# Slot finding moved ahead of the first expert of a routed network, two of four shared-expert groups moved behind the last, and GpSimd's indirect DMAs issued by TensorE's step count

## The chip, the core and the metric

One core of a Trainium2 chip runs the whole program. The metric is the device time of one execution in microseconds (us), the median of three runs. The engines are TensorE (PE in the rows, its weight loads PEld), VectorE (DVE), ScalarE (ACT), GpSimd (POOL) and SyncE (SP, which issues most DMAs); each runs its own instruction list, and they meet through semaphores.

## What is computed

2048 tokens (8 sequences of 256, width 128) go through four stages, each with a LayerNorm behind it. The change touches the second, a mixture of experts:

```python
shared_out = swiglu(x, shared_w1, shared_w2)             # every token
gates = softmax(x @ wg.T)                                # 64 experts
w_topk, idx_topk = top_k(gates, 8)                       # 8 experts of each token, weights normalised
rank = place of the token among those of its expert      # in token order; kept if rank < 160
out = einsum(x1 * silu(x2), expert_w2), x1, x2 = split(buf @ expert_w1)   # buf: 64 experts x 160 slots x 128
x = layernorm(x + shared_out + sum of the kept rows, each times its weight)
```

The first stage is linear attention with running sums, the third four encoder layers, the fourth a block applied to the 192 best-scored of each 256 tokens. Everything is float32, with float16 for the exact small integers of the routing.

## The kernel before

**Stage 1 with the routing in it.** The tokens are handled in 4 groups of 512 (`GROUPS`), 4 tiles of 128 each. While TensorE and VectorE do the attention of group g, the routing of groups g-1 and g-2 is put between: logits (`route_logits`), best eight (`best_of`), masks, ranks (`ranks`, `split_ranks`). The last group's routing comes behind the attention. In the same place the shared expert runs: `shared_hidden(g, f)` on TensorE (L647, L648: two 512-column products for one of 3 blocks of one of 4 groups), Silu and a copy on ScalarE (`shared_halves`, L1056, L1057), the product on GpSimd (`shared_products`, L1298), and `shared_rows(g)` (L659, 24 matmul records), kept by ScalarE (L1061). The first expert waits for all four groups of it (L782).

**Finding slots.** For each set of 4 experts (a "Q", 16 of them) VectorE makes one-hot tables: `low_table` (L1629, 2048 float16 a partition) and `high_table` (three operations of 320: L1635, L1637, L1639). TensorE multiplies them for two Qs at a time (`find_slots`, L721, 64 matmuls), and VectorE turns the result into row numbers (`indices`, L1645 to L1655), which GpSimd's DMAs use. Q 0 to 5 have their tables, and Q 0 to 3 their indices, ahead of the first expert; the rest is done in the experts' loop: a table behind each step's product, and `find_slots` and `indices` in steps 1, 5, 9, 13, 17 and 21.

**The loop of 64 experts** (L785 on TensorE, L1127 on ScalarE, L1700 on VectorE). Step n of TensorE: the result of expert n-2 (`expert_result`, L778, 3 matmuls), one transposition (inputs of the next Q, `turn_inputs`, L748, in the second and third step of a Q; results of an earlier one, `turn_results`, L762, in the others), then the hidden layer of expert n (`expert_hidden`, L768, 6 matmuls, 12 records), which raises the semaphore `expert_mm`. That semaphore releases ScalarE's Silu (L1119), VectorE's copies (L1669) and SP's load of a later expert's weights (L441, 576 KB, a ring of 8). VectorE multiplies (L1681), which releases TensorE's result of that expert two steps later.

GpSimd carries the rows by indirect DMA, 5 blocks of 128 rows for each Q: `gather_block` (L1311) brings tokens and gates from DRAM into one of 4 buffers, `scatter_block` (L1318) puts weighted results (`rows_back`, L1692) back into DRAM. Its list is fixed: gathers of Q 0 to 5 first (`AHEAD = 6`), then, for each Q, five scatters of Q and five gathers of Q+6, one behind the other:

```python
for Q in range(NEG):
    for b in range(RB):
        scatter_block(Q, b)         # waits for back_read at b = 0 and 3
    if Q + AHEAD < NEG:
        for b in range(RB):
            gather_block(Q + AHEAD, b)
```

For Q 10 to 15 no gather is left; four of them have an addition of shared rows and tokens instead (L1344). `rows_back(Q, 0)` waits until the scatters of Q-3 have landed.

**Behind the loop** SP waits for all scatters and loads the returned rows (L453), VectorE and GpSimd sum them (L1738, L1439), and stage 3 begins.

## Time and profile before

| | us |
|---|---|
| three runs | 756.96, 752.38, 752.27; median 752.38 |
| the profiled execution's own time | 748.92 |
| its span, first to last instruction | 747.1 |
| TensorE busy | 583.6 (78%), mean granted clock 0.895 |
| VectorE, GpSimd, ScalarE busy | 454.8, 359.2, 235.2 |
| the loop of experts | about 162.5 to 406.4 of the span |

The chain of work that ended last is 58% TensorE, 15% VectorE, 8% "issue" (waiting for nothing that the profile shows) and 7% "another core or an unknown queue"; the kernel has one core, so the last name means a wait that ended on something that the records don't name. A busy share is an average over stages with different limits: what the change is worth has to be read from the stretches that it touches. Ends of matmuls are modelled.

### The profile page before, as it was taken

Reading aid. Unit: us, or ns where it says so; the run is one execution under the profiler, and the core shown is the slowest. Engines: PE = TensorE matmul, PEld = TensorE weight load, DVE = VectorE, ACT = ScalarE, POOL = GpSimd, SP = SyncE. Lnnn points to the kernel's source line nnn. Section 1 sums busy time; section 2 is a strip of 40 time slices with the busy share of each in tenths; the row PEclk is TensorE's granted clock in tenths of the full one; section 3 lists DMA queues with packets and bytes.
Section 4 is the critical chain, followed back from the end, with each engine's and each line's share of the span. In section 5 each row is a group of like instructions: output and inputs, shape, how many; then the busy total and the mean of one; then the engine's idle time right before and its main releaser. Section 6 shows DMA issues by size and latency. Waiting matters only on the chain.

```text
span 747.1 us, 11154 instructions
## 1 busy us (share of the span) xinstructions
PE 583.6 (78%) x3747; PEld 485.0 (65%) x3747; DVE 454.8 (61%) x1401; ACT 235.2 (31%) x447; POOL 359.2 (48%) x357
## 2 busy tenths in 40 slices
PE   6998877967958697979797032579999999999861
PEld 5767644666958586878796022458777877877641
DVE  4677655616646333323343268887778778777995
ACT  3133245212212122212232010134344344443564
POOL 4655122775465555666456449742243233234342
PEclk9998998879989899889899555689999999999995
DMA  8950000125555566657573660000000000000001
GB/s 306 415 218 22 22 8 21 43 64 180 155 183 170 178 202 202 212 187 236 194 226 95 254 267 1 0 1 12 4 29 11 4 28 11 4 28 1 1 2 57
DMA packets 29565, 79.43 MB, mean 106 GB/s; under 512 B 7104, under 2 KB 12096, under 8 KB 29264
## 3 DMA queue, kind: packets, MB, share of 16 engines
q1 hardware_dynamic: 23088, 65.69, 25.6%
q0 software_dynamic: 6432, 13.16, 6.0%
q8 instruction: 25, 0.41, 0.2%
q14 instruction: 20, 0.16, 0.1%
HBM read 62.60 MB, written 16.25 MB: 106 GB/s over the span
## 4 chain that ended last, share of the span: by engine, by line
PE 58%; DVE 15%; issue 8%; another core or an unknown queue 7%; ACT 4%; POOL 4%; DMA 2%; SPq 0%; DVEq 0%; POOLq 0%; ACTq 0%
PE bank L768 12%; PE bank L904 6%; PE bank L892 6%; PE bank L778 5%; PE bank L525 4%; PE bank L834 3%; PE bank L852 2%; PE bank L815 2%; PE bank L829 2%; DVE stats L253 2%; PE bank L843 2%; PE bank L870 2%; POOL rstd L268 2%; PE bank L557 1%
## 5 line engine op out<-in xcount | busy, mean ns | idle before, releaser
L268 POOL TENSOR_TENSOR rstd<-veps,minus_half 128x4 f32<-128x4 f32 x52 | 53.9, 1037 | 208.0 <-DVE veps L261 205.7
L768 PE MATMUL bank<-hidden,ring 128*128 128x160 f32 x768 | 126.7, 316 | 3.7 <-issue 2.6
L1318 POOL DMA_INDIRECT returned_rows<-x1t,scatter_all x80 | 81.0, 1013 | 81.7 <-DVE x1t L1692 62.5
L768 PEld LDWEIGHTS bank<-hidden,ring 128*128 128x128 f32 x768 | 116.5, 205 | 5.2 <-issue 3.7
L1119 ACT ACTIVATE hidden<-bank 128x480 f32<-128x480 f32 x64 | 36.9, 576 | 185.7 <-PE bank L768 136.3
L778 PE MATMUL bank<-hidden,ring 128*128 128x160 f32 x384 | 68.4, 315 | 19.7 <-DVE hidden L1681 16.4
L778 PEld LDWEIGHTS bank<-hidden,ring 128*128 128x128 f32 x384 | 58.3, 199 | 24.0 <-DVE hidden L1681 19.1
L1669 DVE COPY hidden<-bank 128x384 f32<-128x384 f32 (+1 forms) x32 | 23.3, 732 | 78.1 <-PE bank L768 55.1
L1170 ACT ACTIVATE arena<-bank,layer_cols 128x512 f32<-128x512 f32 x64 | 44.0, 687 | 62.6 <-PE bank L892 62.6
L815 PE MATMUL bank<-consts,arena 128*128 128x128 f32 x192 | 28.4, 284 | 44.1 <-DVE arena L292 44.1
L904 PE MATMUL bank<-ring,arena 128*128 128x128 f32 x512 | 59.9, 275 | 1.4 <-issue 1.4
L904 PEld LDWEIGHTS bank<-ring,arena 128*128 128x128 f32 x512 | 58.4, 192 | 2.4 <-issue 2.4
L892 PE MATMUL bank<-arena,ring 128*128 128x512 f32 x128 | 57.6, 592 | 0.0
L815 PEld LDWEIGHTS bank<-consts,arena 128*128 128x128 f32 x192 | 23.0, 145 | 47.3 <-DVE arena L292 41.5
L1681 DVE TENSOR_TENSOR hidden<-bank,hidden 128x480 f32<-128x480 f32 x64 | 41.8, 654 | 11.0 <-ACT hidden L1119 6.0
L1692 DVE TENSOR_TENSOR x1t<-bank,slot_gate 128x384 f32<-128x384 f32 (+1 forms) x32 | 15.5, 488 | 44.9 <-remote 28.5
L292 DVE TENSOR_SCALAR arena<-shared,mv,rstd 128x128 f32<-128x128 f32 x128 | 38.0, 360 | 7.8 <-POOL rstd L268 7.8
L1266 POOL TENSOR_TENSOR arena<-arena 128x512 f32<-128x512 f32 x30 | 32.7, 1127 | 12.5 <-DVE arena L1474 12.5
L892 PEld LDWEIGHTS bank<-arena,ring 128*128 128x128 f32 x128 | 23.2, 190 | 23.4 <-issue 23.3
L525 PEld LDWEIGHTS bank<-consts,arena 128*128 128x128 f32 x256 | 31.9, 201 | 7.2 <-issue 3.8
L1483 DVE TENSOR_TENSOR arena<-bank,arena 128x512 f32<-128x512 f32 x36 | 24.3, 685 | 19.8 <-PE bank L525 13.8
L1138 ACT ACTIVATE arena<-bank,layer_cols 128x512 f32<-128x512 f32 x16 | 12.4, 777 | 74.4 <-PE bank L815 74.4
(210 smaller groups left out, 1195.0 us busy)
## 6 DMA issues: line engine op xcount, KB each, us to landing
ring<-in_ew SPq DMA_DIRECT2D x64, 576.0 KB
returned_rows<-zeros SPq DMA_DIRECT2D x16, 512.0 KB, 14.9
arena<-returned_rows SPq DMA_DIRECT2D x6, 512.0 KB, 11.8
hidden<-returned_rows SPq DMA_DIRECT2D x4, 512.0 KB, 5.0
ring<-returned_rows SPq DMA_DIRECT2D x4, 512.0 KB, 7.9
ring<-in_l1w SPq DMA_DIRECT2D x8, 256.0 KB, 2.7
returned_rows<-x1t,scatter_all POOLq DMA_INDIRECT x80
shared<-in_xr SPq DMA_DIRECT2D x1, 1024.0 KB, 7.9
```

What stands on the lines that cost most here:

```text
L268: pool.tensor_tensor(rstd[:, s, :], veps[:, s, :], minus_half[:], ALU.pow).then_inc(sem(f"rstd{which}_ready"), 1)
L292: ins = v.tensor_scalar(dst[:, i, :], src[:, i, :], mv[:, s, i, 0:1], rstd[:, s, i:i + 1], ALU.subtract, ALU.mult)
L525: mm = pe.matmul(bank[3 + c % 3][:, tile_of(t)], A["kvp"][:, g % 2, t, P * e:P * e + P], cum, start=True, stop=True)
L768: mm = pe.matmul(bank[2 * (n % 2) + part][:, CAP * f:CAP * f + CAP], ring[:, n % RING, P * (FB * part + f):P * (FB * part + f) + P], E["xt ...
L778: mm = pe.matmul(bank[4 + n % 2][:, 0:CAP], ring[:, n % RING, P * (2 * FB + f):P * (2 * FB + f) + P], E["prod"][:, n % 2, CAP * f:CAP * f ...
L815: mm = pe.transpose(bank[b][:, P * t:P * t + P], src[:, t, :], ident)
L892: pe.matmul(bank[(3, 4, 6, 7)[f]][:], w_up[:, P * f:P * f + P], B["ht"][:, g], start=True, stop=True).then_inc(sem("up_mm"), 1)
L904: mm = pe.matmul(bank[5][:, P * t:P * t + P], B["relu"][:, g % 2, f, P * t:P * t + P], w_down[:, P * f:P * f + P], start=(f == 0), stop=(f ...
L1119: act.activation(E["silu"][:, n % 2, :], bank[2 * (n % 2) + 1][:, 0:FB * CAP], ACT.Silu).then_inc(sem("silu_ready"), 1)
L1170: act.activation(B["relu"][:, g % 2, f], bank[(3, 4, 6, 7)[f]][:], ACT.Relu, bias=layer_col(l, 5 + f)).then_inc(sem("relu_ready"), 1)
L1318: pool.indirect_dma_start(returned_dram[:, :], bass.IndirectOffsetOnAxis(ap=scatter_all[:, Q, b:b + 1], axis=0), E["back"][:, Q % BACK, b, ...
L1681: v.tensor_tensor(E["prod"][:, n % 2, :], bank[2 * (n % 2)][:, 0:FB * CAP], E["silu"][:, n % 2, :], ALU.mult).then_inc(sem("prod_g_ready"), 1)
```

## The change

1. All slots are found ahead of the first expert, in 5 calls (`FOUND`: one pair of Qs, one pair, then two pairs three times). The high tables are made in two wide calls (Qs 0 and 1; Qs 2 to 15) from codes and token numbers that ScalarE spreads out beforehand, in place instead of by way of `here`. The low tables of Qs 0 to 3 are made for the first 12 of 16 tiles while the last group's logits are under way. The loop loses its tables, its `find_slots` and its `indices`.
2. The shared expert: groups 0 and 1 stay ahead of the loop (`SOON = 2`), with the product on VectorE straight from PSUM instead of copy and GpSimd; groups 2 and 3 come behind the loop, and their bases are added by VectorE instead of GpSimd. `shared_hidden(0, 0)` moves behind the last group's attention.
3. GpSimd's list waits for TensorE's steps.

```diff
-        here = sb("here", [2, RB, TILES, EG], F16)
-        a_code, b_code, token16 = sb("a_code", [RA * EG], F16), sb("b_code", [RB * EG], F16), sb("token16", [TILES], F16)
+        a_code, b_code = sb("a_code", [RA * EG], F16), sb("b_code", [RB * NE], F16)
+        token16 = hidden[:, 3 * FB - 1].bitcast(F16)
...
+        SOON = 2
+        late = [B["kp"][:, m] for m in range(GROUPS)] + [B["eq"][:, m] for m in range(2)]
...
+        FOUND = ((0,), (1,), (2, 3), (4, 5), (6, 7))
...
-                if g == GROUPS - 1:
-                    shared_hidden(0, 0)
...
             attention_out(GROUPS - 1, 1)
+            shared_hidden(0, 0)
             shared_hidden(0, 1)
+            turn_x1(GROUPS - 1)
+            route_logits(GROUPS - 1)
             shared_hidden(0, 2)
-            turn_x1(GROUPS - 1)
+            ranks(GROUPS - 1)
             shared_hidden(1, 0)
-            route_logits(GROUPS - 1)
             shared_hidden(1, 1)
-            ranks(GROUPS - 1)
...
+            find_slots(0)
             shared_rows(0)
             shared_hidden(1, 2)
...
+            find_slots(1)
             shared_rows(1)
+            for call in range(2, len(FOUND)):
+                find_slots(call)
...
-            pe.wait_ge(sem("shared_ready"), GROUPS)
+            pe.wait_ge(sem("shared_ready"), SOON)
...
                 expert_hidden(n).then_inc(sem("expert_mm"), 1)
-                if j == 1 and Q + 2 < NEG // 2:
...
-                    find_slots(Q + 2, bank[6])
...
+            for g in range(SOON, GROUPS):
+                turn_late(g)
+            for f in range(FB):
+                late_hidden(SOON, f)
+            late_hidden(SOON + 1, 0)
+            late_rows(SOON)
+            late_hidden(SOON + 1, 1)
+            late_hidden(SOON + 1, 2)
+            late_rows(SOON + 1)
...
-            for b in range(RB):
-                gather_block(0, b)
-            shared_products(2)
-            for b in range(RB):
-                gather_block(1, b)
-            shared_products(3)
-            for Q in range(2, AHEAD):
+            for Q in range(AHEAD):
                 for b in range(RB):
                     gather_block(Q, b)
             pool.wait_ge(sem("zeroed"), 16 * TOK * TOPK // (8 * P))
+            def step(n):
+                pool.wait_ge(sem("expert_mm"), min(n + 1, NE + LAG))
+
             for Q in range(NEG):
-                for b in range(RB):
+                n = EG * Q + 2 * EG
+                step(n)
+                for b in (0, 1):
+                    scatter_block(Q, b)
+                step(n + 1)
+                for b in (2, 3, 4):
                     scatter_block(Q, b)
                 if Q + AHEAD < NEG:
-                    for b in range(RB):
+                    step(n + 2)
+                    for b in (0, 1):
                         gather_block(Q + AHEAD, b)
-                elif Q + AHEAD < NEG + GROUPS:
...
+                    step(n + 3)
+                    for b in (2, 3, 4):
+                        gather_block(Q + AHEAD, b)
```

VectorE's list ahead of the loop becomes, from the last residual on:

```diff
+            shared_product(0)
+            shared_product(1)
+            v.wait_ge(sem("codes_ready"), 2)
+            v.wait_ge(sem("bi_ready"), GROUPS - 2)
+            for Q in range(4):
+                low_table(Q, 0, KNOWN)
             best_of(GROUPS - 1)
             masks_of(GROUPS - 1)
             places_of(GROUPS - 1)
             split_ranks(GROUPS - 1)
+            v.wait_ge(sem("b_index"), GROUPS)
+            v.tensor_copy(group_of(bi16, GROUPS - 1), group_of(logits_i, GROUPS - 1)).then_inc(sem("bi_ready"), 1)
             invert_sums(GROUPS - 1)
...
+            high_tables(0, 2)
+            for Q in (0, 1):
+                low_table(Q, KNOWN)
+            indices(0)
+            for m in (2, 3, 4):
+                shared_product(m)
+            high_tables(2, NEG)
+            for Q in (2, 3):
+                low_table(Q, KNOWN)
+            low_table(4)
+            indices(1)
+            shared_product(5)
+            for call in (2, 3, 4):
+                for Q in range(4 * call - 4, 4 * call):
+                    if Q > 4:
+                        low_table(Q)
+                if call > 2:
+                    indices(call - 1)
+            indices(4)
```

Behind its last `rows_back`, VectorE adds the bases of groups 0 and 1, makes the 6 products of the late groups (`late_product`) and adds their bases; ScalarE has 2 copies and 6 Silus there, where it had none.

## Rows read from the trace of the kernel before

**Rows 1.** Stretches between Silus of steps 0, 8, 50, then loop end, scatters landed, rows in.
```profile
core 0: us, PE busy (x) PEld busy (x) DVE busy (x) ACT busy (x) POOL busy (x), PEclk, DMA share, GB/s
165.49:196.36 30.87, 25.25 (x219) 24.31 (x219) 19.12 (x45) 6.71 (x14) 12.34 (x13) 0.93 0.48 150
196.36:367.82 171.46, 135.70 (x991) 129.55 (x991) 69.16 (x152) 37.70 (x84) 104.80 (x105) 0.90 0.62 194
367.82:406.40 38.58, 37.72 (x281) 37.02 (x280) 17.15 (x34) 13.88 (x30) 20.64 (x20) 1.00 0.50 158
406.40:417.90 11.50, 0.02 (x1) 0.00 (x0) 0.73 (x2) 0.00 (x0) 7.86 (x8) 0.61 0.51 164
417.90:425.50 7.60, 0.00 (x0) 0.00 (x0) 0.65 (x6) 0.00 (x0) 0.00 (x0) 0.50 0.88 326
```

**Rows 2.** Stretch view of four steps, 368.79 to 379.67, with five scatters in them.
```profile
368.79:379.67 10.88, 10.88 (x84) 10.88 (x83) 4.77 (x10) 3.33 (x8) 6.22 (x6) 1.00 0.76 249
```

**Rows 3.** Waits of 196.36 to 367.82: engine line waited for, us, times, longest.
```profile
ACT hidden L1119 <- PE bank L768: 85.9, 25, 11.7
ACT hidden L1119 <- remote: 47.9, 10, 7.6
```

**Rows 4.** Timeline of all engines, 284 to 304 (start us, us, engine, line, operation).
```profile
288.28 1.80 PE L768 MATMUL bank<-hidden,ring 128*128 128x160 f32 x12
290.95 1.80 PE L768 MATMUL bank<-hidden,ring 128*128 128x160 f32 x12
293.22 0.95 POOL L1311 DMA_INDIRECT small<-dispatch_rows,gather_all  x1 [0.30 <-issue]
295.91 0.57 ACT L1119 ACTIVATE hidden<-bank 128x480 f32<-128x480 f32 x1 [7.63 <-remote]
297.23 1.97 PE L778 MATMUL bank<-hidden,ring 128*128 128x160 f32 x6 [4.48 <-DVE hidden L1681]
297.28 1.02 POOL L1318 DMA_INDIRECT returned_rows<-x1t,scatter_all  x1 [3.11 <-DVE x1t L1692]
299.63 3.41 PE L768 MATMUL bank<-hidden,ring 128*128 128x160 f32 x12
301.19 0.98 POOL L1318 DMA_INDIRECT returned_rows<-x1t,scatter_all  x1 [0.30 <-issue]
302.48 0.98 POOL L1318 DMA_INDIRECT returned_rows<-x1t,scatter_all  x1 [0.30 <-issue]
```

**Rows 5.** Timeline of GpSimd, the first scatter of the runs before and after.
```profile
281.65 1.02 POOL L1318 DMA_INDIRECT returned_rows<-x1t,scatter_all  x1 [3.25 <-DVE x1t L1692]
312.97 1.02 POOL L1318 DMA_INDIRECT returned_rows<-x1t,scatter_all  x1 [3.18 <-DVE x1t L1692]
```

**Rows 6.** Timeline, 97 to 162: what stands ahead of the loop.
```profile
99.15 1.05 PE L525 MATMUL bank<-consts,arena 128*128 128x128 f32 x8
100.24 0.69 DVE L1483 TENSOR_TENSOR arena<-bank,arena 128x512 f32<-128x512 f32 x1 [1.99 <-PE bank L525]
116.09 0.60 DVE L1519 MAX8 best<-logits 128x8 f32<-128x64 f32 x4 [7.87 <-ACT logits L1029]
123.44 2.09 DVE L1629 TENSOR_TENSOR arena<-zeros,a_code 128x2048 f16<-128x2048 f16 x1 [2.74 <-ACT zeros L1048]
154.51 5.40 PE L659 MATMUL bank<-sw,hidden 128*128 128x128 f32 x24 [4.35 <-POOL hidden L1298]
161.19 1.24 DVE L1669 COPY hidden<-bank 128x384 f32<-128x384 f32 x2 [12.76 <-issue]
```

**Rows 7.** The lines of the tables and of the shared hidden layer: ns min/median/max.
```profile
L1629 DVE TENSOR_TENSOR arena<-zeros,a_code x16: 1214/1216/2092, 123.4 to 242.3; 128x2048 f16<-128x2048 f16 x16
L1635 DVE TENSOR_TENSOR here<-zeros,b_code x16: 301/315/1380, 125.5 to 245.3; 128x320 f16<-128x320 f16 x16
L1637 DVE TENSOR_TENSOR arena<-here,token x16: 491/492/503, 126.9 to 245.7; 128x320 f16<-128x320 f16 x16
```

**Rows 8.** Timeline, 402 to 426: the end of the loop and what follows.
```profile
402.72 0.57 ACT L1119 ACTIVATE hidden<-bank 128x480 f32<-128x480 f32 x1 [0.92 <-PE bank L768]
415.64 0.98 POOL L1318 DMA_INDIRECT returned_rows<-x1t,scatter_all  x1 [0.30 <-issue]
425.53 3.69 DVE L1738 TENSOR_TENSOR hidden<-hidden 128x1536 f32<-128x1536 f32 x2 [6.86 <-DMA hidden<-returned_rows]
```

**Rows 9.** Timeline: a shared hidden product and the rows of a group, full clock.
```profile
136.83 1.02 PE L648 MATMUL bank<-x1t,sw 128*128 128x512 f32 x2
137.69 1.02 PE L647 MATMUL bank<-x1t,sw 128*128 128x512 f32 x2
143.78 2.94 PE L659 MATMUL bank<-sw,hidden 128*128 128x128 f32 x24 [1.70 <-POOL hidden L1298]
```

More of the change, by code:

```diff
@@ new lines, in find_slots @@
+            def find_slots(call):
+                if call >= 2:
+                    pe.wait_ge(sem("slots_read"), call - 1)
+                if call == 1:
+                    pe.wait_ge(sem("hidden_ready"), 4)
+                for k, q in enumerate(FOUND[call]):
+                    pe.wait_ge(sem("one_hots_ready"), 2 * q + 2)
+                    for u in range(2):
+                        at = 2 * RB * EG * (2 * k + u)
+                        lo = EG * (2 * q + u)
+                        for i in range(TILES):
+                            mm = pe.matmul(slot_bank(call)[:, at:at + 2 * RB * EG], a16[:, i, 2 * q + u, :],
+                                           b16[:, :, i, lo:lo + EG], start=(i == 0), stop=(i == TILES - 1))
+                mm.then_inc(sem("slots_mm"), 1)
@@ L1132, in _ @@
                     keep_result(n - LAG)
+            for g in range(SOON, GROUPS):
+                act.wait_ge(sem("turned_x1"), GROUPS + g - SOON + 1)
+                act.activation(B["ht"][:, g], bank[4 + g % 2][:], ACT.Copy).then_inc(sem("x1t_ready"), 1)
+            for m in range(FB * SOON, FB * GROUPS):
+                act.wait_ge(sem("hidden_mm"), m + 1)
+                act.activation(late[m - FB * SOON], bank[2 * (m % 2) + 1][:], ACT.Silu).then_inc(sem("hidden_read"), 1)
             def norm1_columns(n, g, l):
@@ L1642, in indices @@
-            def indices(q, to):
-                qs = slice(2 * q, 2 * q + 2)
-                v.wait_ge(sem("slots_mm"), q + 1)
-                v.tensor_tensor(picked[:], to[:, 0:4 * RB * EG].rearrange("p (u b e) -> p u b e", u=2, e=EG),
-                                own.unsqueeze(1).unsqueeze(1).to_broadcast([P, 2, 2 * RB, EG]), ALU.mult).then_inc(
-                    sem("slots_read"), 1)
-                v.wait_ge(sem("slots_read"), q + 1)
-                ch.after(ch.did(v.tensor_reduce(slots[:, qs].rearrange("p g t b -> p g (t b)"), picked[:], AX.X, ALU.add)))
+            KNOWN = GT * (GROUPS - 1)
@@ new lines, in low_table, with high_tables @@
+            def low_table(Q, first=0, last=TILES):
+                n = last - first
+                ins = v.tensor_tensor(a_out[:, first:last, Q],
+                                      a_in[:, first:last, EG * Q:EG * Q + EG].unsqueeze(2).to_broadcast([P, n, RA, EG]),
+                                      codes_a.unsqueeze(1).to_broadcast([P, n, RA, EG]), ALU.is_equal)
+                if last == TILES:
+                    ins.then_inc(sem("one_hots_ready"), 1)
+            def high_tables(first, last):
+                es, n = slice(EG * first, EG * last), EG * (last - first)
+                wide = [P, RB, TILES, n]
+                hit = b_out[:, 0:RB, :, es]
+                ch.after(ch.did(v.tensor_tensor(hit, b_in[:, :, es].unsqueeze(1).to_broadcast(wide),
+                                                codes_b[:, :, es].unsqueeze(2).to_broadcast(wide), ALU.is_equal)))
+                ch.after(ch.did(v.tensor_tensor(b_out[:, RB:2 * RB, :, es], hit,
+                                                place[:, :, es].unsqueeze(1).to_broadcast(wide), ALU.mult)))
+                ch.after(ch.did(v.tensor_tensor(hit, hit, token[:, :, es].unsqueeze(1).to_broadcast(wide), ALU.mult)))
@@ new lines, in indices @@
+            def indices(call):
+                n = 2 * len(FOUND[call])
+                qs = slice(2 * FOUND[call][0], 2 * FOUND[call][0] + n)
+                v.wait_ge(sem("slots_mm"), call + 1)
+                v.tensor_tensor(picked[:, 0:n], slot_bank(call)[:, 0:2 * RB * EG * n].rearrange(
+                    "p (u b e) -> p u b e", u=n, e=EG), own.unsqueeze(1).unsqueeze(1).to_broadcast([P, n, 2 * RB, EG]),
+                    ALU.mult).then_inc(sem("slots_read"), 1)
+                v.wait_ge(sem("slots_read"), call + 1)
+                ch.after(ch.did(v.tensor_reduce(slots[:, qs].rearrange("p g t b -> p g (t b)"), picked[:, 0:n], AX.X,
+                                                ALU.add)))
@@ L1723, in _, with add_base, late_product @@
                 rows_back(NEG - 1, c)
+            def add_base(g):
+                if g < SOON:
+                    v.wait_ge(sem("shared_ready"), g + 1)
+                    rows = tiles(shared, g)
+                else:
+                    v.wait_ge(sem("shared_mm"), g + 1)
+                    rows = bank3(4 + g % 2)
+                v.tensor_tensor(tiles(shared, g), rows, tiles(x1, g), ALU.add).then_inc(sem("base_ready"), 1)
+            def late_product(m):
+                v.wait_ge(sem("hidden_read"), m + 1)
+                v.tensor_tensor(late[m - FB * SOON], bank[2 * (m % 2)][:], late[m - FB * SOON], ALU.mult).then_inc(
+                    sem("hidden_ready"), 1)
+            for g in range(SOON):
+                add_base(g)
+            for m in range(FB * SOON, FB * SOON + 4):
+                late_product(m)
+            add_base(SOON)
+            for m in range(FB * SOON + 4, FB * GROUPS):
+                late_product(m)
+            add_base(SOON + 1)
             v.wait_ge(sem("consts_in"), 16)
```

186 lines of the change are left out of this document (73 added, 113 removed).

## The prediction

> **What bounds the kernel now.** I read the page first, then the stretch view along the loop, then the waits and the timeline of one stall. The page shows TensorE busy for 78% of the span and heading the chain, so the loop of 64 experts looks like TensorE's. The stretch view says otherwise. In steps 50 to 54 TensorE is busy for the whole of 10.88 us at full clock, 2.72 us a step [rows 2]. Steps 8 to 50 take 171.46 us, 4.08 a step, with TensorE busy for 135.7 of it [rows 1]; 42 steps at 2.72 would be 114.2. So 57 us are lost there, and 9 more in steps 0 to 8 (30.87 against 8 x 2.72 = 21.8) [rows 1].
>
> The waits of steps 8 to 50 tell who waits, not why: ScalarE 85.9 us for TensorE's hidden layer (L768) and 47.9 us for "remote", which no record names [rows 3]. The timeline shows one such stall. TensorE's hidden layer of step 31 starts at 288.28 and ends by its record at 290.08, the next starts at 290.95, yet ScalarE's Silu starts only at 295.91, and the product and with it TensorE's next result at 297.23 [rows 4]. TensorE had done two layers whose semaphores had reached nobody. What ran meanwhile is GpSimd's list of five scatters and five gathers, 1.29 us apart, from 281.65 to 294.17 [rows 4, 5]; the release comes 2.69 us after the start of its last gather, and there are ten such runs, one for each Q. In all of them the last semaphore is let go in this way. Behind the stall the next hidden layer takes 3.41 us instead of 1.80 [rows 4], so part of it is paid again at half clock (mean 0.90 in this stretch, 1.00 in the next [rows 1]). Steps 50 to 63 have runs of five scatters only and keep 2.72 a step [rows 2]. So what ends last in the loop is a wait tied to long runs of indirect DMAs; the start of a run (281.65, 297.28, 312.97) repeats every 15.7 us [rows 4, 5], where TensorE needs 10.9.
>
> **The change, part by part**, against the profiled execution's 748.9 us; the median of the runs, 752.4, is 3.5 above it, added at the end.
>
> *Ahead of the loop.* Three things make the tables start earlier. `shared_hidden(0, 0)` goes from the last attention's chain: VectorE's idle 1.99 us at 100.24 is its price [rows 6], so -2.0. A shared block (two products at 0.86, their spacing [rows 9]) leaves the way of the last logits, -1.7. VectorE waits 2.74 us for ScalarE's copy of the high bits [rows 6] and now makes it itself in about 0.3, -2.4. The four partial low tables (0.75 x 1.22 = 0.9 each [rows 7]) fill the 7.87 us in which VectorE waits for the logits [rows 6] and cost nothing; without that cover, 3.7. First table: 123.4 - 6.1 = 117.3. From there VectorE's list runs alone: high tables of Qs 0 and 1 1.4, two quarter tables 0.8, waiting for `find_slots` 1.3, five `indices` at about 1.1 5.5, four products at 0.7 2.8, the wide high tables 3 x 4480 elements at 0.59 ns (the rate of L1629 [rows 7]) 7.9, two quarter tables 0.8, twelve low tables 14.4, the last wait 0.5: 35.4 us, ending at 152.7. The first columns were copied at 161.19 [rows 6], and there the kernel waited not for tables but for the shared expert, whose GpSimd products stood between gathers (TensorE idle 4.35 us before the last L659 [rows 6]). So finding all slots first costs nothing here: -8.5 us. Bounds: if the wide tables run at L1637's 1.54 ns an element [rows 7], 12.8 us more and a start at +4.3; if all goes well, -11. I take the rate of L1629, since the wide tables, like it, read a last dimension that isn't spread from one value.
>
> The first tables took 2.09 and 1.38 us where others take 1.2 and 0.3 [rows 7], both while GpSimd multiplied; the products leave GpSimd, and no gather slowed a low table this much. The Trainium skill, SBUF — State Buffer, "Who interferes with whom", says that a two-input VectorE operation contends with GpSimd operations that read SBUF, not with those that only write it. By it the tables beside gathers keep their speed, and a case in which all twelve take 2.09 (10 us more) is excluded; I keep that case inside the bound above.
>
> *Steps 0 to 8.* Six `find_slots` and all tables leave the loop. Here two waited on an `indices` held up by a run of gathers. 21.8 us, plus 1.6 for a first step at half clock: 23.4, -7.5. Bounds 0 (gathers of Q 4 and 5 still run here) and -9.
>
> *Steps 8 to 50.* GpSimd has 10 x 1.29 = 12.9 us of work for a Q, against TensorE's 10.9. Its list is now let go in twos and threes by steps 4Q+8 to 4Q+11. As soon as it lags (at once: three DMAs take 3.9 us, a step 2.7), a gate is already open when it gets there, and the list runs on without gaps, as now. But a held-up semaphore now also stops GpSimd, after at most a few DMAs instead of ten, so the hold ends sooner. What is queued behind a gate on GpSimd is only its own DMAs: scatters of Q are needed by `rows_back(Q+3)` at step 4Q+19, gathers of Q+6 by step 4Q+21, ten steps later, so the later start is covered; without that cover each gate would cost up to 2.7. Bounds of the length of a Q: below, 10.9 (no hold left; 42 steps 114.2, -57.3); above, today's 171.46 / 10.5 = 16.3, or 18.5 (last rival). I take 13.3, just above GpSimd's own 12.9: TensorE is then held to GpSimd's pace. 10.5 x 13.3 = 139.7, -31.8.
>
> *Steps 50 to the end.* TensorE is already at its pace: 38.58 us stay [rows 1].
>
> *The late groups.* TensorE does 6 shared blocks (1.72 each), two sets of rows (2.94 each [rows 9]), transpositions and first Silu 2, exposed products 2: 20.2 us, ending near 426.6; VectorE's last base follows at 428. It lies where VectorE waited from 407 to 425.53 for returned rows [rows 1, 8]: +2.5. Bounds 0 and +19 (all of it at half clock).
>
> The sum: -8.5 - 7.5 - 31.8 + 2.5 = -45.3, so 703.6 for the profiled execution and **707** as median.
>
> **Rivals.**
> *A. The holds vanish* (runs of two and three never hold a semaphore). For: runs of five hardly hold one [rows 2]. Against: GpSimd's runs are only nominally short, as it lags from the first Q on. The loop goes at 2.72; the new bound is GpSimd at the end: 10 x 12.9 + 6 x 6.45 = 167.7 us from step 8 to its last DMA. TensorE's way is 55 x 2.72 + 13.9 (from the last Silu at 402.72 to the last scatter's end at 416.6 [rows 8]) = 163.5, so +4.3; the late groups are covered. -8.5 - 7.5 - 57.3 + 4.3 = -69: **683**.
> *B. The dealing does nothing* (gates are always open, the run stays a run). For: the lag just named. Against: a gate can't be open when its semaphore is what is held. Length of a Q 15.7, the repeat seen without tables [rows 5]: 164.9, -6.6; steps 0 to 8 -4; front and late as above: -16.6: **736**. The Trainium skill, DMA: Bandwidth & Descriptors, "Anatomy of one DMA — SWDGE (gpsimd) path", says that many descriptors can be emitted before their cost shows, and that the fixed cost is completion latency. By it the length of a run is harmless and B is right; the timeline, where the hold ends with the run, speaks against it, and no run here yet shows which.
> *C. Slower: every small run holds a semaphore.* A run of two would then release 1.29 + 2.69 = 3.98 us after its start, one of three 5.27, and, as the next run waits for that release, a Q takes 2 x (3.98 + 5.27) = 18.5 us, and in Qs 10 to 15 3.98 + 5.27 + 5.4 = 14.7. -8.5 - 7.5 + 22.8 + 12.4 + 2.5 = +21.7: **774**. It decides from 17.5 us a Q on. Against it: at full pace five scatters in a row cost nothing [rows 2].
>
> **How the numbers follow.** Chances: forecast 0.5, A 0.28, B 0.14, C 0.05, the front or the late groups far off 0.03. The range goes from just under A to just over B: 681 to 740. Within 1% of 752.4 (745 to 760, about what a measurement tells from no change) lies only B with a bad front or late part: 0.05. Slower by over 1%: C and a part of the rest, 0.06. Faster: 0.89.
>
> **What would show it.** First hidden layer at about 154, not 162.5. Distance from one Q's first scatter to the next: 13 to 14 us (forecast), 10.9 at first with GpSimd never idle (A), 15.7 (B), over 17 (C). "Remote" waits of ScalarE at 10 to 25 us instead of 47.9 in steps 8 to 50. TensorE busy between 406 and 426 of the old timeline, and L1738 late by 2 to 3 us. I am wrong if the tables take over 45 us ahead of the loop, or if the loop's stalls stay where no GpSimd run ends.

## The result, and the profile after

| | before | after |
|---|---|---|
| median of the runs | 752.33 | 722.38 (720.79 to 724.3) |
| profiled execution, its span | 748.92, 747.1 | 723.01, 721.2 |
| ratio of the runs, 95% interval | | 0.958, 0.9533 to 0.9626 |
| TensorE busy, mean granted clock | 583.6, 0.895 | 580.0, 0.919 |

It is 30 us faster, where 45 were forecast (707 in a range of 681 to 740). The ratio is taken from the runs; the quotient of the two medians is 0.960. The line numbers have moved: the experts' hidden layer is L780 (before L768), their result L790 (L778), Silu L1153 (L1119), the product L1743 (L1681), columns L1731 (L1669), `gather_block` L1340, `scatter_block` L1347, the low tables L1659, the high tables L1669 to L1673.

Stretch view of the kernel after, between the Silus of steps 0, 8 and 50, the end of the loop and the first sum of returned rows (start:end, length, then the busy time and count of PE, PEld, DVE, ACT, POOL, the granted clock, DMA share, GB/s), to be read beside [rows 1]:

```profile
156.61:183.24 26.63, 23.02 (x155) 22.29 (x154) 8.63 (x18) 6.56 (x15) 10.86 (x12) 0.93 0.56 176
183.24:338.64 155.40, 125.70 (x861) 119.63 (x859) 51.08 (x104) 37.59 (x85) 99.78 (x103) 0.97 0.65 211
338.64:378.30 39.66, 37.84 (x281) 37.37 (x282) 17.30 (x36) 13.72 (x31) 19.46 (x20) 1.00 0.52 167
378.30:398.45 20.15, 17.27 (x82) 10.51 (x80) 8.07 (x19) 4.67 (x8) 8.67 (x10) 1.00 0.67 230
```

The first Silu comes 8.9 us earlier (156.61, before 165.49). Steps 0 to 8 take 26.6 us (30.9), steps 8 to 50 155.4 (171.5), and the rest up to the first sum 59.8 (57.7). Together -27.1; the span is 25.9 shorter, so 1.2 are given back in the stages behind. Of the 155.4 us TensorE is idle for 29.7: the stalls are still there. ScalarE's waits in that stretch (line, what it waited for: us in total, times, longest), beside [rows 3]:

```profile
ACT hidden L1153 <- PE bank L780: 75.9, 22, 5.4
ACT hidden L1153 <- remote: 39.4, 9, 6.8
ACT hidden L1153 <- issue: 4.2, 1, 4.2
```

The longest wait has gone from 11.7 to 6.8 us, their number from 35 to 32, and their sum from 133.8 to 119.5 us: 14.3 less, nearly all of the 16.1 that the stretch has gained. A large part of what is left is no stall, since the 42 waits of a run without stalls add up to 75.1 us (coarser gates, below). One of the stalls in the timeline of the kernel after (start, duration, engine, line, operation, in brackets the idle time before it and what ended it):

```profile
278.02 0.98 POOL L1347 DMA_INDIRECT returned_rows<-x1t,scatter_all  x1 [2.08 <-PE bank L780]
281.88 0.99 POOL L1340 DMA_INDIRECT arena<-dispatch_rows,gather_all  x1 [0.30 <-PE bank L780]
285.33 1.80 PE L780 MATMUL bank<-hidden,ring 128*128 128x160 f32 x12
286.97 0.95 POOL L1340 DMA_INDIRECT arena<-dispatch_rows,gather_all  x1 [0.30 <-issue]
288.04 0.57 ACT L1153 ACTIVATE hidden<-bank 128x480 f32<-128x480 f32 x1 [5.39 <-PE bank L780]
288.81 1.01 POOL L1347 DMA_INDIRECT returned_rows<-x1t,scatter_all  x1 [0.90 <-PE bank L780]
290.13 1.00 POOL L1347 DMA_INDIRECT returned_rows<-x1t,scatter_all  x1 [0.30 <-issue]
290.84 3.12 PE L780 MATMUL bank<-hidden,ring 128*128 128x160 f32 x12
292.49 0.57 ACT L1153 ACTIVATE hidden<-bank 128x480 f32<-128x480 f32 x1 [3.53 <-remote]
```

At 278.02 a gate had stopped GpSimd for 2.08 us. The gate at 281.88 cost it nothing (0.30 us is the usual gap); it stood open already, and so ten DMAs went out between 278.02 and 290.13, with one pause of 0.9. The gates did not cut the list into twos and threes; they cut it into runs of mostly 7, 8 or 10, and a stall of 5.4 us and one of 3.5 stand where one of 7.6 stood [rows 4].

The front, timeline of VectorE in the kernel after:

```profile
107.69 3.55 DVE L1659 TENSOR_TENSOR arena<-zeros,a_code 128x1536 f16<-128x1536 f16 x4
117.69 0.46 DVE L1669 TENSOR_TENSOR arena<-zeros,b_code 128x640 f16<-128x640 f16 x1
126.37 2.49 DVE L1671 TENSOR_TENSOR arena<-arena,place 128x4480 f16<-128x4480 f16 x1
134.94 8.03 DVE L1659 TENSOR_TENSOR arena<-zeros,a_code 128x2048 f16<-128x2048 f16 x7
151.69 1.23 DVE L1731 COPY hidden<-bank 128x384 f32<-128x384 f32 x2
```

The first table work behind the last logits starts at 117.69 (forecast 117.3), the wide high tables take 2.49 us each for 4480 elements, 0.56 ns an element (0.59 taken), and the first columns are copied at 151.69 (forecast 152.7). The four partial low tables stand where VectorE used to wait for the logits [rows 6]. Low tables beside gathers kept 1.15 us each (8.03 for seven); it is the gathers whose issue took up to 2.86 us there instead of 0.95, as GpSimd's timeline shows (124.30 to 149.6).

The end, timeline of the kernel after:

```profile
397.27 0.69 DVE L1787 TENSOR_TENSOR shared<-bank,x 128x512 f32<-128x512 f32 x1 [3.04 <-PE bank L838]
398.45 4.09 DVE L1816 TENSOR_TENSOR hidden<-hidden 128x1536 f32<-128x1536 f32 x2
```

The last base of the late groups is done (397.96) 0.5 us before the first sum of returned rows (before L1738, 425.53 [rows 8]). The wait for those rows, 6.86 us in [rows 8], is now filled by the late groups.

### The profile page after: what moved, and what is told of

The parts are those of the page before. It is cut to its first block, busy times and chain, and to the rows that moved or that the text cites. A ratio compares the mean times of both kernels' runs of the same rounds, so it can differ in the third digit from the quotient of the medians.

```text
span 721.2 us, 11097 instructions
## 1 busy us (share of the span) xinstructions
PE 580.0 (80%) x3755; PEld 479.8 (67%) x3755; DVE 453.1 (63%) x1362; ACT 230.2 (32%) x434; POOL 345.1 (48%) x341
## 4 chain that ended last, share of the span: by engine, by line
PE 58%; DVE 23%; issue 8%; another core or an unknown queue 4%; POOL 2%; ACT 2%; DMA 1%; SPq 0%; DVEq 0%; ACTq 0%; POOLq 0%
PE bank L780 13%; PE bank L946 6%; PE bank L790 6%; PE bank L934 6%; PE bank L539 4%; PE bank L876 3%; PE bank L894 2%; DVE stats L256 2%; DVE arena L1659 2%; PE bank L857 2%; PE bank L871 2%; DVE hidden L1743 2%; PE bank L885 2%; PE bank L912 2%
## 5 line engine op out<-in xcount | busy, mean ns | idle before, releaser
L780 PE MATMUL bank<-hidden,ring 128*128 128x160 f32 x768 | 123.4, 311 | 4.6 <-issue 2.7
L780 PEld LDWEIGHTS bank<-hidden,ring 128*128 128x128 f32 x768 | 113.4, 200 | 6.5 <-issue 4.3
L1347 POOL DMA_INDIRECT returned_rows<-x1t,scatter_all x80 | 79.3, 991 | 65.9 <-DVE x1t L1754 21.8
L1153 ACT ACTIVATE hidden<-bank 128x480 f32<-128x480 f32 x64 | 36.9, 576 | 177.6 <-PE bank L780 110.5
L790 PE MATMUL bank<-hidden,ring 128*128 128x160 f32 x384 | 66.4, 310 | 31.8 <-DVE hidden L1743 19.1
L790 PEld LDWEIGHTS bank<-hidden,ring 128*128 128x128 f32 x384 | 56.0, 193 | 37.3 <-DVE hidden L1743 22.8
L1731 DVE COPY hidden<-bank 128x384 f32<-128x384 f32 (+1 forms) x32 | 22.9, 719 | 66.3 <-PE bank L780 33.9
L1211 ACT ACTIVATE arena<-bank,layer_cols 128x512 f32<-128x512 f32 x64 | 44.0, 687 | 62.6 <-PE bank L934 62.6
L946 PEld LDWEIGHTS bank<-ring,arena 128*128 128x128 f32 x512 | 58.4, 192 | 2.4 <-issue 2.4
L1743 DVE TENSOR_TENSOR hidden<-bank,hidden 128x480 f32<-128x480 f32 x64 | 41.7, 652 | 13.1 <-ACT hidden L1153 7.5
L539 PEld LDWEIGHTS bank<-consts,arena 128*128 128x128 f32 x256 | 31.8, 200 | 7.5 <-issue 4.2
L1513 DVE TENSOR_TENSOR arena<-bank,arena 128x512 f32<-128x512 f32 x36 | 24.4, 685 | 18.1 <-PE bank L539 12.2
L876 PEld LDWEIGHTS bank<-ring,arena 128*128 128x128 f32 x128 | 26.9, 210 | 13.0 <-issue 9.9
```

Source lines behind the costliest of these rows:

```text
L539: mm = pe.matmul(bank[3 + c % 3][:, tile_of(t)], A["kvp"][:, g % 2, t, P * e:P * e + P], cum, start=True, stop=True)
L780: mm = pe.matmul(bank[2 * (n % 2) + part][:, CAP * f:CAP * f + CAP], ring[:, n % RING, P * (FB * part + f):P * (FB * part + f) + P], E["xt ...
L790: mm = pe.matmul(bank[4 + n % 2][:, 0:CAP], ring[:, n % RING, P * (2 * FB + f):P * (2 * FB + f) + P], E["prod"][:, n % 2, CAP * f:CAP * f ...
L876: mm = pe.matmul(bank[3 + h][:, 2 * D * t:2 * D * t + 2 * D], B["ht"][:, g, P * (2 * h + t):P * (2 * h + t) + P], w_qkv[:, P:3 * P], start ...
L946: mm = pe.matmul(bank[5][:, P * t:P * t + P], B["relu"][:, g % 2, f, P * t:P * t + P], w_down[:, P * f:P * f + P], start=(f == 0), stop=(f ...
L1211: act.activation(B["relu"][:, g % 2, f], bank[(3, 4, 6, 7)[f]][:], ACT.Relu, bias=layer_col(l, 5 + f)).then_inc(sem("relu_ready"), 1)
```

## The experiments

The runs fell on four chips, here called I to IV in order of time, each with runs of the kernel before beside them. Those gave medians of 754.8, 696.1, 751.4 and 695.4 us: two kinds of chip, of which I knew nothing before chip II. Each chip was used in one stretch of time only, so a passing state of the machine is not told apart from the chip. The first measurement (752.3 and 722.4), whose chip is not on record, is of the slower kind.

Two words are used for short. A *hold* is a stall in which a semaphore of TensorE's matmuls reaches nobody for some us after the matmuls have ended by their (modelled) records. A *gate* is a wait of GpSimd for a step of TensorE. In the edits, "..." stands for lines left out.

### Chip I: the kernel before at 754.8

**Without the gates.** The kernel after, GpSimd's list as in the kernel before:

```diff
 for Q in range(NEG):
-    n = EG * Q + 2 * EG
-    step(n)
-    for b in (0, 1):
-        scatter_block(Q, b)
-    step(n + 1)
-    for b in (2, 3, 4):
+    for b in range(RB):
         scatter_block(Q, b)
... (the gathers likewise)
```

> The changed kernel with part 3 undone: GpSimd's list has no gates, five scatters and five gathers in a row. My theory (a gate stops GpSimd as soon as a semaphore is held, so holds end sooner): a Q in the loop takes 15.7 us again where it took 14.8 in the changed kernel, 9 to 10 us more in all, so about 732. Rival B (the dealing does nothing, the gain is that tables and slot finding left the loop): 722, within 0.5% of the changed kernel. Rival D (dealing hurts, since it starts scatters and gathers later): 715 or less.

Measured: 730.44 us, ratio 0.9699 (0.9612 to 0.9785). Its stretch from step 8 to step 50:

```profile
185.80:350.10 164.30, 134.46 (x863) 127.25 (x862) 52.39 (x104) 37.66 (x84) 101.92 (x104) 0.92 0.63 203
```

164.3 us, 15.65 a Q, with runs of exactly ten DMAs 15.8 us apart. So the first two parts of the change give about 24 us on this chip, and the gates the rest. How much that is depends on the comparison, since the kernel with gates was not run on this chip: 8.1 us by its first median (722.4) and 10.1 by that on chip III (720.4), but 5.6 and 6.6 when each is set against the kernel before beside it (30.0 and 31.0 gained, less 24.4), and 9 by the ratios. The intervals of the ratios, 0.9612 to 0.9785 here and 0.9533 to 0.9626 with gates, overlap slightly. So 6 to 10 us, and the sign is surer than the size.

**The gates alone.** The kernel before, with the gates of the kernel after and nothing else:

```diff
...
 for Q in range(NEG):
-    for b in range(RB):
+    n = EG * Q + 2 * EG
+    step(n)
+    for b in (0, 1):
+        scatter_block(Q, b)
+    step(n + 1)
+    for b in (2, 3, 4):
         scatter_block(Q, b)
... (the gathers likewise)
```

> The kernel before with part 3 alone: same gates by step count, tables and slot finding still in the loop. My theory: 752 less 9 to 12 us, 740 to 743, since the runs of ten are cut by gates there too. Rival B: 752, within 0.5%. If it is slower than 752, the gates cost more than they give when indices come late.

Measured: 745.82 us, ratio 0.9905 (0.9857 to 0.9953). Steps 8 to 50 of its trace:

```profile
193.80:363.90 170.10, 137.34 (x1010) 130.79 (x1008) 68.86 (x153) 38.04 (x85) 107.81 (x106) 0.93 0.62 197
```

170.1 us where the kernel before has 171.5 [rows 1] and, in a second trace on chip III, 176.1. The total is about one per cent lower: more than nothing, less than I expected.

**Without the gathers.** The kernel after without the gathers of Qs 6 to 15 (those experts compute on old rows), so five scatters a Q are left:

```diff
...
-    if Q + AHEAD < NEG:
-        step(n + 2)
-        ...
```

TensorE's wait for a gather is set to those that are still made.

> The changed kernel without the gathers of Q 6 to 15: later experts work on rows of earlier ones, so 50 of 160 indirect DMAs are left out. If holds need more than five or so indirect DMAs in a row (my theory), the loop keeps 2.72 us a step from step 8 on and steps 8 to 50 take 114 to 118 us instead of 155: about 683. If scatters alone hold semaphores too, or the holds come from the weight loads, the loop keeps at least half of its stalls: over 700.

Measured: 685.13 us. Steps 8 to 50, and ScalarE's waits in them:

```profile
185.00:299.30 114.30, 114.30 (x864) 114.30 (x863) 53.97 (x105) 39.13 (x85) 52.82 (x54) 1.00 0.80 248
```

```profile
ACT hidden L1153 <- PE bank L780: 68.2, 38, 2.1
```

TensorE is never idle, at full clock, and no wait is longer than 2.1 us; 42 steps in 114.3 are 2.72 each. All stalls of steps 8 to 50 hang on the gathers being there, by their kind or by making ten DMAs a Q out of five. The opening gathers are still there, the last 12 of them 1.25 us apart (149.7 to 163.4), and so is their stall: the Silu of step 1 comes 9.0 us behind that of step 0.

**Without the weights.** The kernel after without SP's loads of the weights of experts 8 to 63 (they compute with the first eight experts' weights), to see whether the stalls come from crowded DMA engines:

```diff
-for n in range(RING, NE):
-    sp.wait_ge(sem("expert_mm"), n - RING + LAG + 1)
-    sp.dma_start(ring[:, n % RING, :], ew[n]).then_inc(sem(f"expert_in{n % RING}"), 16)
... (TensorE waits for the first load of each place in the ring only)
```

> The changed kernel without the weight loads of experts 8 to 63 (they use the first eight's weights): 33 MB less traffic in the loop, the same indirect DMAs. If a semaphore is held by GpSimd's runs alone (my theory), the stalls stay: steps 8 to 50 within 10 us of 155, total 712 to 722. If it takes indirect DMAs and weight loads together (rival E: crowding of the DMA engines), the stalls go and the loop runs at GpSimd's or TensorE's pace: 683 to 700.

Measured: 722.02 us; steps 8 to 50 and ScalarE's waits (Silu is L1150 there):

```profile
181.80:338.90 157.10, 132.97 (x863) 125.75 (x862) 51.72 (x105) 37.76 (x85) 101.62 (x104) 0.92 0.19 54
```

```profile
ACT hidden L1150 <- remote: 52.0, 12, 6.3
```

The DMA engines' share falls from 0.65 to 0.19, the stretch stays at 157 us. Crowding by the weights is not the cause.

### Chip II: the kernel before at 696.1

Here the kernel before is 56 us faster than on chip I, though nothing in it is changed. The four kernels were made for a chip like the first; what they show is something else.

**Coarser gates**, five and five:

```diff
     step(n)
     for b in (0, 1):
         scatter_block(Q, b)
-    step(n + 1)
     for b in (2, 3, 4):
         scatter_block(Q, b)
     ...
-        step(n + 3)
```

> The kernel after with coarser gates: five scatters at step 4Q+8, five gathers at step 4Q+10, instead of twos and threes by each step. My theory (a held semaphore stops GpSimd at the next gate, so the nearer the gates, the shorter the run that holds): runs of five and ten, worth between no gates (730.4) and four gates (722.4): about 726. Rival (a five never holds, and the gate between the fives is as good as four): 720 to 722 or less, as each five then starts in a gap. Rival (gates only help by their number, a gate passed in a burst helps nothing): 730.

Measured: 678.27 us, ratio 0.9752 (0.9701 to 0.9802). Stretches of steps 0 to 8, 8 to 50 and 50 to 63:

```profile
156.30:176.80 20.50, 20.50 (x155) 20.50 (x154) 8.93 (x18) 6.74 (x15) 11.27 (x12) 1.00 0.74 227
176.80:291.00 114.20, 114.20 (x863) 114.20 (x862) 53.93 (x104) 39.12 (x84) 86.58 (x89) 1.00 0.90 279
291.00:327.80 36.80, 35.27 (x264) 34.84 (x264) 15.44 (x30) 12.11 (x26) 27.96 (x30) 1.00 0.60 197
```

Its timeline of GpSimd, the first scatter and the last one of the loop, and ScalarE's waits of steps 8 to 50:

```profile
177.61 1.02 POOL L1347 DMA_INDIRECT returned_rows<-x1t,scatter_all  x1 [6.69 <-DVE x1t L1752]
343.59 0.98 POOL L1347 DMA_INDIRECT returned_rows<-x1t,scatter_all  x1 [0.30 <-issue]
```

```profile
ACT hidden L1153 <- PE bank L780: 75.1, 42, 1.9
```

Between 177.61 and 343.59 stand 130 indirect DMAs without a gap over the usual one, as long as any run in these traces, and nothing is held in steps 8 to 50: 42 waits, none over 1.9 us, TensorE at full clock and never idle. On this chip a long run holds no semaphore. The gates are open whenever GpSimd comes to them, since it lags from the first Q on. What bounds the loop's end is GpSimd: one step (57) waits 1.8 us more than the others. None of the three theories is told apart by the time, since all of them spoke of holds.

**The opening gathers dealt out.** The kernel after with the gathers of Qs 3, 4 and 5 dealt by steps 0 to 5:

```diff
 for Q in range(AHEAD):
     for b in range(RB):
+        if Q >= DEALT and b in (0, 2):
+            step(2 * (Q - DEALT) + b // 2)
         gather_block(Q, b)
```

> The kernel after, with the opening gathers of Qs 3, 4 and 5 (15 DMAs) dealt out too: two and three by steps 0 to 5. In the kernel after they stand in one run of 12 and one of 5 (149.9 to 173.9), and steps 0 to 8 take 26.6 us where eight undisturbed steps take 21.8. My theory: the run of 12 is what holds step 1 for 6.2 us; dealt out, steps 0 to 8 take 22 to 24 us and the total falls by 3 to 5, to 718. Rival (GpSimd only lags more and pays it in the Qs behind): 722, no change. Rival (gathers of Q 3 become late for the columns of step 9, or the later start of the list moves all scatters back): 725 or more.

Measured: 678.49 us, ratio 0.9748 (0.9695 to 0.9801): the same as the coarser gates. Steps 0 to 8 take 20.6 us here and 20.5 there, where all 30 opening gathers stand in one run, the last 17 of them 1.25 us apart from 150.0 on. There was nothing to win.

**Without the scatters** of Qs 0 to 9 (their rows do not come back to the tokens):

```diff
-    step(n)
-    ...
+    if Q >= SENT:          # SENT = 10
+        step(n)
+        ...
```

> The kernel after, with the scatters of Qs 0 to 9 left out (their rows never reach DRAM); GpSimd keeps its gates and has five gathers for each Q in the loop. It is the counterpart of the run without gathers (685.1, no stall at 2.72 us a step). My theory (the number of indirect DMAs back to back holds TensorE's semaphores, whatever their kind): no stall either, steps 8 to 50 in 114 to 120 us, total 685 to 690. Rival (it is the gathers, which write SBUF, that hold; scatters are harmless): stalls stay, steps 8 to 50 in 140 us or more, total above 705.

Measured: 674.85 us, steps 8 to 50 in 114.3. That fits my theory by its numbers and proves nothing, since here ten a Q don't hold either.

**Landings instead of steps.** The kernel after, its gates replaced by waits for GpSimd's own DMAs:

```diff
     for b in range(RB):
         scatter_block(Q, b)
+    pool.wait_ge(sem(f"scattered{Q % BACK}"), 16 * RB * (Q // BACK + 1))
     if Q + AHEAD < NEG:
         for b in range(RB):
             gather_block(Q + AHEAD, b)
+        pool.wait_ge(sem(f"gathered{(Q + AHEAD) % GOT}"), 16 * RB * ((Q + AHEAD) // GOT + 1))
```

> The kernel after without the gates on TensorE's steps; instead GpSimd waits, behind each five scatters and behind each five gathers, until they have landed, so that ten in a row become two fives with a gap of the landing time (about 2 us). My theory (only more than about five back to back hold a semaphore): no stall of more than about 3 us in steps 8 to 50, but a Q takes GpSimd 2 x (5 x 1.29 + 2) = 16.9 us at most, 15 at least; total 722 to 745, set by GpSimd's pace with ScalarE's waits spread out. Rival (a semaphore is held whenever indirect DMAs are in flight): each Q has two stalls in place of one and the total is above 745. Rival (the gap lets everything through, and five need less than I think): 14 us a Q, below 720.

Measured: 746.79 us, 50.7 more than the kernel before on this chip. GpSimd's timeline, the last of five scatters, the first and the last of five gathers, and the first scatter of the next Q:

```profile
278.09 0.98 POOL L1347 DMA_INDIRECT returned_rows<-x1t,scatter_all  x1 [0.30 <-issue]
282.67 0.99 POOL L1340 DMA_INDIRECT small<-dispatch_rows,gather_all  x1 [3.60 <-DMA returned_rows<-x1t,scatter_all]
287.76 0.95 POOL L1340 DMA_INDIRECT small<-dispatch_rows,gather_all  x1 [0.30 <-issue]
291.22 1.01 POOL L1347 DMA_INDIRECT returned_rows<-x1t,scatter_all  x1 [2.51 <-DMA small<-dispatch_rows,gather_all]
```

I had taken 2 us for a landing; in this Q it takes 2.5 behind the gathers and 3.6 behind the scatters, over all Qs 2.4 to 4.9 and 1.6 to 4.1. This Q takes 291.22 - 272.89 (its first scatter) = 18.3 us, and once the six Qs of lead are used up TensorE waits for gathers (the columns of the next Q), up to 5.7 us at a time; ScalarE's longest wait for a hidden layer is 10.0. This is the case in which GpSimd's list is the bound, and it shows what a gate costs that really stops it: the margin is 12.9 us of work a Q against TensorE's 10.9, so there is none.

### Chip III: the kernel before at 751.4

To settle whether the chip or the kernels made the difference, the kernel after and the kernel before, both unchanged:

> The kernel after, unchanged, beside the kernel before on the chip of this call. The last four runs were made on another chip than the first ones: there the kernel before took 696 us instead of 752 to 755, and in the trace of the run with coarser gates 130 indirect DMAs in one go from 177.6 to 343.6 held nothing. Theory H (the holds come with the chip; the length of a run decides only where they occur): the two kernels' times go by whether this chip has holds. If the kernel before takes 745 to 760 here, the kernel after takes about 722 and has stalls; if it takes 690 to 700, the kernel after has none and takes about 678, front -8.5, steps 0 to 8 about 0 to -3, steps 8 to 50 0, end GpSimd-bound. Rival (the coarser gates and the dealt opening brought the 678, the chip only the rest): above 685 where the kernel before takes 696.

Measured: 720.35 us, ratio 0.9600 (0.9549 to 0.9651). Steps 8 to 50 and ScalarE's waits:

```profile
183.10:339.30 156.20, 129.31 (x871) 124.74 (x870) 51.78 (x104) 37.58 (x84) 102.29 (x105) 0.93 0.66 214
```

```profile
ACT hidden L1153 <- remote: 30.4, 7, 7.6
```

> The kernel before, unchanged, for its trace on the chip of this call. Theory H: if its time here is 690 to 700, its ten runs of ten indirect DMAs stand in the trace as before and no Silu waits more than 3 us between steps 8 and 50, which then take 114 to 118 us; if its time is 745 to 760, 171 us with ten stalls. Rival (the stalls stand there at 696 too, and what differs is another stage): 171 us with a total of 696.

Measured: 751.59 us. Its steps 8 to 50:

```profile
195.10:371.20 176.10, 134.69 (x996) 129.60 (x996) 68.83 (x153) 37.77 (x85) 103.19 (x105) 0.91 0.60 190
```

176 us, with up to 13.8 from one Silu to the next. This chip has the holds, and both kernels repeat their first measurement in time. The stretch itself differs by 4.6 us between the two traces of the same kernel, so a split of a few us that rests on one trace each is not firm.

### Chip IV: the kernel before at 695.4

> The kernel after without the scatters of Qs 0 to 9, once more: its first run (674.85 us, no stall) was on the chip on which no kernel shows a hold, so it told nothing of them. If the kernel before takes 745 to 760 on this chip: my theory (the count of indirect DMAs in one go holds, whatever their kind) gives steps 8 to 50 in 114 to 120 us and a total near 685; the rival (gathers hold, scatters do not) 140 us or more and above 705. If the kernel before takes 690 to 700, about 675 again, and the question stays open.

Measured: 677.69 us. A chip without holds once more, so this run leaves the question of the kind of DMA open. The traces from the slower kind of chip answer a part of it all the same, since they have runs of one kind at both ends of the loop. In the kernel after (first measurement), TensorE's layer of step 5 beside five gathers alone (168.95 to 174.88), and its last rows of group 2 beside the last ten scatters alone (376.19 to 388.96):

```profile
172.14 1.80 PE L780 MATMUL bank<-hidden,ring 128*128 128x160 f32 x12
176.07 0.57 ACT L1153 ACTIVATE hidden<-bank 128x480 f32<-128x480 f32 x1 [3.95 <-remote]
386.60 2.84 PE L838 MATMUL bank<-sw,arena 128*128 128x128 f32 x24
390.63 0.69 DVE L1787 TENSOR_TENSOR shared<-bank,x 128x512 f32<-128x512 f32 x1 [2.51 <-PE bank L838]
```

The layer ends at 173.94 and its Silu starts 2.1 us later. The rows end at 389.44 and VectorE starts 1.2 us later (1.1 to 1.2 in all five traces of the slower kind that have this tail), while the four Silus that fall into the first part of the scatters keep the spacing that they have on chip II. With the coarser gates on chip II the same two instructions stand 0.04 us apart:

```profile
339.64 2.84 PE L838 MATMUL bank<-sw,arena 128*128 128x128 f32 x24
342.52 0.69 DVE L1785 TENSOR_TENSOR shared<-bank,x 128x512 f32<-128x512 f32 x1 [1.35 <-PE bank L838]
```

So gathers alone hold, and ten scatters alone hold too, but later and shorter. Even five scatters alone do: in the kernel before the layer of step 62 ends at 399.9 and its Silu starts at 400.87, 1.0 us late. Steps of 2.72 us absorb that.

> The kernel after with the gathers of Qs 3, 4 and 5 dealt out by steps 0 to 5, once more. On a chip with holds (the kernel before at 745 to 760): my theory, the opening run of 12 holds steps 1 to 4, and dealing it out brings steps 0 to 8 from 27 to 28 us down to 22 to 24 and the total from 721 to 717; rival, the same DMAs only hold later, and the total stays at 720 to 723; rival, it comes out above 725 since the list lags into the first scatters. On a chip without (690 to 700): 678.5 again, as for the coarser gates.

Measured: 677.61 us, ratio 0.9728 (0.9693 to 0.9762), steps 0 to 8 in 20.6 us and 130 DMAs in one go, as on chip II. Whether dealing out the opening gathers helps on a chip with holds was not measured: both runs of it fell on chips without.

## Why the prediction was right or wrong

**The front** (-8.5): -8.9, and by the steps that were named: table work from 117.7, wide tables at the rate of L1629, first columns at 151.7. On chips II and IV the first Silu starts between 154.0 and 156.3.

**Steps 0 to 8** (-7.5): -4.2. I gave a first step at half clock and nothing else; the gathers that still run there stood in the bound of 0 and not in the term. What was missed is the stall behind the opening gathers: 25 of them in one run, the last 12 at 1.25 us each, the last issued at 163.6, and the Silu of step 1 comes 6.2 us behind that of step 0 (9.0 in the run without gathers in the loop, 2.0 on chip II). It is the same hold that I had read out of [rows 4] for the loop; I did not apply it to the list in front of it.

**Steps 8 to 50** (-31.8): -16.1, and this is the term that failed. It alone is 15.7 us off, about what the forecast of 707 missed (15.4). That the two agree so closely is chance: the 3.3 us missed in steps 0 to 8 and the 1.2 given back behind are made up by the median, which lies 0.6 us below the profiled execution where 3.5 above were added. The term came from "I take 13.3, just above GpSimd's own 12.9", a length of a Q that let the gates end nearly all holding. Measured are 155.4 / 10.5 = 14.8 us, and ScalarE's "remote" waits are 39.4 us where 10 to 25 were named as the sign. The run without gates splits the term. Tables and slot finding out of the loop: 171.5 to 164.3, -7.2, where rival B had -6.6 for just this (164.9). The gates: 164.3 to 155.4, -8.9, where my sum had 164.9 - 139.7 = 25.2 for them. So the other parts were right, as far as single traces tell (the kernel before has 176.1 in its other trace), and the worth of the gates was nearly three times too high. The wrong step is "the hold ends sooner": a gate that is already open stops nothing, and the timeline shows two of the four gates of a Q open: those of 278.02 and 288.81 stop GpSimd, that of 281.88 and the one behind it do not, since a hold lets two steps' semaphores go together or nearly so. The argument for rival B, which I had set aside with "a gate can't be open when its semaphore is what is held", was half right. A term between two ends that far apart (10.9 and 16.3) would have been better put at their middle, 13.6, or higher, than next to a floor that no row showed being reached.

**Steps 50 to the end and the late groups** (+2.5): +2.1 together, close by its size and by its reason. The last scatter ends at about 389, and the last base ends 0.5 us before the rows are in.

**Rival A** (683, the holds vanish) is what happens on chips II and IV, for a reason that I had not thought of: they have no holds to begin with, so that the kernel before is there at 696 as well. That its 683 lies near the 678 measured there is luck, since it was worked out as 69 us less than 752 and not from a kernel before of 696. Its arithmetic of the new bound holds there: from step 8 to the end of GpSimd's last DMA 167.7 us were worked out, and 343.59 + 0.98 - 176.80 = 167.8 were measured with the coarser gates; the total came out at 678. The change itself was not run on such a chip. Its two neighbours, with coarser gates and with the opening dealt out too, gain 18 us there (2.5 and 2.7%) against the kernel before, in place of 30. For them the gates can't be the cause, as nothing is held; the front's 9 us are probably in it, as the first Silu comes at 154.0 to 156.3 there too, but I have no trace of the kernel before from such a chip to show it or to name the rest.

**Rival B** (736, the dealing does nothing): its trace is the run without gates, 730.4. It was nearer than its chance of 0.14 says. Beside it stood a rule of the Trainium skill, DMA: Bandwidth & Descriptors, "Anatomy of one DMA — SWDGE (gpsimd) path": many descriptors can be emitted before their cost shows. On chips II and IV the traces agree, with 130 in a row at no cost. On the slower kind GpSimd issues the DMAs no more slowly either (0.95 to 1.02 us each in the loop), but what I had concluded from the rule, that the length of a run is harmless, fails: there the gathers cost 722.4 - 685.1 = 37 us, by other engines' waits.

**Rival C** (774, every small run holds): small runs do hold a semaphore, five gathers for 2.1 us and five scatters for 1.0, but at 2.72 us a step that costs next to nothing: the run without gathers has 114.3 us for steps 8 to 50 with scatters in it.

**What was right in the reading**: that the loop's stalls hang on runs of indirect DMAs and not on TensorE, which only the run without gathers could show; that the weights' traffic has no part in it; that the late groups lie in a wait. What none of these runs settles is what in a chip (or in the state of the machine at the time) makes the holds, by what mechanism a run of DMAs keeps a semaphore back, and why gathers do it sooner than scatters.

## What to carry to other kernels

Price a throttle by what is waiting when it is reached: a gate on a semaphore that arrives in bursts is mostly open, and it shortens a run only where the engine behind it is ahead, not where it lags. Before you tune against a stall that no record names, measure the unchanged kernel on a second chip; here 56 us of 752 went with the chip, and, going by the two kernels nearest to the change, about 12 of the 30 us that it gained. And when a mechanism is found in one stretch (a run of DMAs that holds semaphores), look for it in every other stretch where the same pattern stands, the opening gathers here.

## What the runs showed of the hardware

- The same program takes 751 to 755 us on two chips and 695 to 696 on two others, each run within 1% of its chip's median. On the first kind a semaphore of TensorE's matmuls that comes due beside a run of GpSimd's indirect DMAs can be kept back, the last ones of a run mostly until 1.0 to 2.8 us behind its end: 5.8 us by a run of ten (290.08 to 295.91 [rows 4]), 2.1 by five gathers, 1.0 by five scatters. On the second kind the Silu starts 0.04 us behind the end of its layer, at 62 of the 64 steps with 130 in a row (coarser gates; near the two others matmul records are missing).
- A hold costs twice, first as a wait, then as a lower clock: the stretch of the run without gates has a granted clock of 0.92 and 134 us of TensorE's time for work that takes 114 at full clock (1.00, no idle) in the run without gathers.
- Five indirect DMAs, waited for until they have landed, need 2.4 to 4.9 us (gathers) or 1.6 to 4.1 us (scatters) behind the end of the last one, in the run with waits for landings, against 1.3 us from the start of one to the start of the next when nobody waits.
- VectorE's product of 4480 float16 elements whose inputs have a last dimension that isn't spread from one value (L1671) takes 2.49 us, 0.56 ns an element, about a third of the 1.54 ns that L1637 took with 320 elements in the kernel before [rows 7]. Length and layout of the input differ at once, so which of them does it isn't shown.
